# Five gathered columns of each run pass are fetched row by row from SyncE's queue

## The reference, cut to what matters

```python
pooled = jax.ops.segment_max(h[edge_src], edge_dst, num_segments=N)   # three times, first network
agg = jax.ops.segment_sum(msgs, dst, num_segments=n_nodes)            # two types of edge, third network
m = jax.ops.segment_sum(hW[edge_type, src], dst, num_segments=num_nodes)  # eight types, fourth network
```

## Time and profile before

| | |
|---|---|
| time, median of 3 runs | 4963.57 us (4955.61 to 4965.45) |
| the profiled execution's own time | 4973.72 us |
| its span | 4972.0 us |
| GpSimd busy | 3199.0 us (64% of the span) |
| VectorE busy | 2845.9 us (57%) |
| TensorE matmuls busy | 3481.2 us (70%) |

### The profile page before, as it was taken

The page is one execution under the profiler, slowest core; times in us unless marked ns, Lnnn a source line. Parts: engine busy times, 40 slices in busy tenths (PEclk is TensorE's granted clock), DMA queues, the critical chain, the costliest instruction groups (busy, mean ns, idle before and its releaser), DMA issues.

```text
span 4972.0 us, 70678 instructions
## 1 busy us (share of the span) xinstructions
PE 3481.2 (70%) x18022; PEld 2634.2 (53%) x18022; DVE 2845.9 (57%) x8726; ACT 2119.5 (43%) x4948; POOL 3199.0 (64%) x3257
## 2 busy tenths in 40 slices
PE   3122189979999688788888888887889987962100
PEld 2011178867788565556655565555778873431000
DVE  6754334436444688787888878787544442124433
ACT  1000068955788343335333353333479974420000
POOL 4777677766767377774777747776057772027776
PEclk7555599989999899999999999999999998985555
DMA  5556566665656433333333333333166662246665
GB/s 181 192 171 215 193 201 221 222 206 186 203 197 228 147 104 104 104 105 97 103 105 105 104 92 104 104 105 106 64 205 214 213 213 75 102 150 207 206 204 190
DMA packets 275492, 776.56 MB, mean 156 GB/s; under 512 B 63777, under 2 KB 99874, under 8 KB 270882
## 3 DMA queue, kind: packets, MB, share of 16 engines
q0 software_dynamic: 155568, 425.01, 29.9%
q1 hardware_dynamic: 119538, 347.03, 18.2%
HBM read 454.85 MB, written 316.93 MB: 155 GB/s over the span
## 4 chain that ended last, share of the span: by engine, by line
PE 34%; DMA 9%; POOL 9%; issue 6%; DVE 5%; ACT 2%; DVEq 1%; SPq 0%; POOLq 0%; ACTq 0%
PE PS L1157 9%; PE PS L1363 8%; POOL HC L539 5%; PE PS L1355 5%; PE PS L1289 3%; DMA X<-table,idx_src 3%; PE PS L1050 3%; DMA HC<-table_typ,run_typ 3%; DMA HC<-table,idx_src 2%; POOL HC L515 2%; POOL X L515 1%; DVE work L1985 1%; PE PS L1344 1%; PE PS L1452 1%; PE PS L1044 1%
## 5 line engine op out<-in xcount | busy, mean ns | idle before, releaser
L1798 DVE SCALAR_TENSOR_TENSOR HC<-HC,run_rst 128x256 f32<-128x256 f32 x1858 | 901.9, 485 | 930.3 <-DMA HC<-table,run_max 288.3
L539 POOL DMA_INDIRECT HC<-table,run_max x1101 | 1088.7, 989 | 462.2 <-issue 288.1
L515 POOL DMA_INDIRECT HC<-table,idx_src x648 | 639.1, 986 | 352.6 <-DMA table<-B 156.0
L1157 PE MATMUL PS<-AM,ring 128*128 128x256 f32 x3600 | 794.9, 384 | 26.7 <-ACT ring L738 21.9
L1157 PEld LDWEIGHTS PS<-AM,ring 128*128 128x128 f32 x3600 | 692.8, 193 | 129.0 <-DVE HC L1798 23.3
L515 POOL DMA_INDIRECT X<-table,idx_src x600 | 602.9, 1005 | 182.9 <-issue 128.0
L1355 PE MATMUL PS<-AM,work 128*128 x3744 | 648.8, 285 | 20.5 <-DVE score L1985 19.1
L2041 DVE SCALAR_TENSOR_TENSOR HC<-HC,fcol,PS 128x257 f32 x1248 | 586.0, 470 | 102.6 <-PE PS L1363 91.2
L539 POOL DMA_INDIRECT HC<-table_typ,run_typ x391 | 379.0, 969 | 396.2 <-DMA table_typ<-HC 277.3
L539 POOL DMA_INDIRECT HC<-table_rel,run_rel x371 | 360.6, 972 | 283.0 <-DMA table_rel<-B 170.2
L1355 PEld LDWEIGHTS PS<-AM,work 128*128 128x128 bf16 x3744 | 373.9, 101 | 224.2 <-issue 72.6
(11 more groups left out here) (270 smaller groups left out, 5640.2 us busy)
## 6 DMA issues: line engine op xcount, KB each, us to landing
prefix<-HC SPq DMA_DIRECT2D x485, 512.0 KB, 3.4
table_typ<-HC SPq DMA_DIRECT2D x18, 1024.0 KB, 3.8
HC<-table,run_max POOLq DMA_INDIRECT x1101, 3.3
HC<-table,idx_src POOLq DMA_INDIRECT x648, 2.8
X<-table,idx_src POOLq DMA_INDIRECT x600, 2.8
HC<-table_typ,run_typ POOLq DMA_INDIRECT x391, 2.9
table_typ<-AM SPq DMA_DIRECT2D x6, 1024.0 KB, 3.8
HC<-table_rel,run_rel POOLq DMA_INDIRECT x371, 3.3
```

Source lines behind the costliest of these rows:

```text
L515: pool.indirect_dma_start(held(t)[:, 0:D], None, table, bass.IndirectOffsetOnAxis(ap=idx_src[:, t:t + 1], axis=0)).then_inc(landed[t % AHE ...
L539: pool.indirect_dma_start(run_slot(k), None, src, bass.IndirectOffsetOnAxis(ap=run_idx[s[1]][:, j:j + 1], axis=0)).then_inc(landed[k], 16)
L1157: last = nc.tensor.matmul(PS[:, (2, 5)[c % 2], h * D:(h + 1) * D], duos(s)[:, x % 4, b % 2, h * P:(h + 1) * P], rows, start=(b + h == 0), ...
L1798: V.scalar_tensor_tensor(run_slot(k), run_slot((j - 1) % SLOTS), run_rst[:, j:j + 1], fresh, fade, join).then_inc(pooled, 1)
```

## The change

In every run stage, five columns (89, 162, 235, 308, 381) are no longer gathered by GpSimd. SP fetches each of them with 128 DMAs of one row, 1 KB, whose address in the table comes from a register. The registers are loaded 32 at a time from a list of row numbers that is kept on one partition. Seven such rows are issued ahead of each write of running rows, from turn 1 on, so a stage's 640 rows are out after 92 turns. A fetched column goes to one of three homes outside the 24 slots, and VectorE waits for its 128 landings, 16 counts each, before it combines it. For "rel" and "typ" SP loads two lists at the stage's start and VectorE computes the row numbers out of them with two small instructions before its first column.

```diff
+BY_SP = [89 + 73 * i for i in range(5)]
+BITE = 32
+A_TURN = 7
...
+def fetched_in(s):
+    return [] if s[0] != "runs" else BY_SP
...
+        def fetch(eng, n, rows, js, free):
+            s = PLAN[n]
+            for i, j in enumerate(js):
+                if i >= free:
+                    eng.wait_ge(pooled, before(n, ("runs",)) * TILES + js[i - free] + 1)
+                for p in range(0, P, BITE):
+                    regs = nc.values_load_multi_w_load_instructions(
+                        single_src[s[1]][0:1, bass.ds(fetched_in(s).index(j) * P + p, BITE)], engines=(eng.engine,), min_val=0,
+                        max_val=rows.shape[0] - 1, skip_runtime_bounds_check_because="the indices are the graph's own")[1]
+                    for k in range(BITE):
+                        eng.dma_start(single_home(s, j)[p + k:p + k + 1, :], rows[bass.ds(regs[k], 1), :]).then_inc(x_in[single_sem(j)], 16)
+                        yield
...
-                        if j in picked_in(s):
+                        if j in picked_in(s) + fetched_in(s):
                             continue
                         pool.indirect_dma_start(
...
+                    if s[1] == "rel":
+                        sp.wait_ge(rel_tabled[0], 16 * REL2 * 4)
+                        sp.wait_ge(rel_tabled[1], 16 * REL2 * 2)
+                    elif s[1] == "typ":
+                        for k in range(WIDES):
+                            sp.wait_ge(wided[k], ...)
+                    if s[1] != "max":
+                        kind = 1 if s[1] == "rel" else 2
+                        sp.dma_start(single_src[s[1]], singles[0:1, :]).then_inc(loaded, 16)
+                        sp.dma_start(single_type.bitcast(I32), singles[kind:kind + 1, :]).then_inc(loaded, 16)
+                    one_by_one = fetch(sp, n, {"max": table, "rel": table_rel, "typ": table_typ}[s[1]], BY_SP, 3)
                     for g in range(TURNS):
+                        if g == 1 and s[1] == "max":
+                            sp.wait_ge(loaded, 16 * 7)
+                            sp.wait_ge(tabled, 16 * PARTS * tables(n))
+                        elif g == 1:
+                            sp.wait_ge(keys_made, 2 if s[1] == "rel" else 3)
+                        if g >= 1:
+                            for _ in range(A_TURN):
+                                next(one_by_one, None)
                         while s[1] == "max" and far < len(pairs_in(s)) and pairs_in(s)[far][0] // 4 - 9 <= g:
...
+                        elif j in fetched_in(s):
+                            g = j // 4
+                            dve.wait_ge(written[g % TEAMS], 16 * (drained(n, g % TEAMS) + g // TEAMS))
+                            dve.wait_ge(x_in[single_sem(j)], x_count(n, single_sem(j), j))
+                            fresh = single_home(s, j)
```

More of the change, by code:

```diff
@@ L118, in duos_in, with gnn_kernel @@
     return -(-tabled_in(s) // 2)
-def gnn_kernel(nc, edges, runs, picks, rel_picks, xN, weights, biases, bias_rows, out, table, table_rel, table_typ, stash, step_rows, prefix):
+def fetched_in(s):
+    return [] if s[0] != "runs" else BY_SP
+def gnn_kernel(nc, edges, runs, picks, singles, rel_picks, xN, weights, biases, bias_rows, out, table, table_rel, table_typ, stash, step_rows, prefix):
     PLAN = plan()
@@ L252, in run_slot, with single_home, single_sem @@
             return flatC[:, k * D:(k + 1) * D]
+        single_src = {"max": Wfold[:].rearrange("p f c d -> p (f c d)")[0:1, 0:len(BY_SP) * P].bitcast(I32),
+                      "rel": AM[0:1, 35 * D:35 * D + len(BY_SP) * P].bitcast(I32)}
+        single_src["typ"] = single_src["rel"]
+        single_type = AM[0:1, 8 * D:8 * D + len(BY_SP) * P]
+        def single_home(s, j):
+            k = BY_SP.index(j) % 3
+            at = 32 * D if s[1] != "max" else 25 * D
+            return work[:, 1024 + k * D:1024 + (k + 1) * D] if s[:3] == ("runs", "max", 1) else AM[:, at + k * D:at + (k + 1) * D]
+        def single_sem(j):
+            return BY_SP.index(j) % 3
         def halves(v):
@@ L413, in columns, with x_count @@
         def columns(s, k, upto=TILES):
-            return sum(1 for j in range(k, upto, SLOTS) if j not in picked_in(s)) if k < SLOTS else 0
+            return sum(1 for j in range(k, upto, SLOTS) if j not in picked_in(s) + fetched_in(s)) if k < SLOTS else 0
+        def x_count(n, k, j=-1):
+            return 16 * sum({"start": 1, "attention": s[-1] == LAYERS - 1, "runs": P * sum(1 for f in fetched_in(s) if single_sem(f) == k)}.get(s[0], 0)
+                            for s in PLAN[:n]) + 16 * P * sum(1 for f in fetched_in(PLAN[n]) if single_sem(f) == k and f <= j)
         def own_bank(s, b):
@@ L522, in _ @@
                         pool.wait_ge(tabled, 16 * PARTS * tables(n))
-                        pool.wait_ge(loaded, 16 * 6)
+                        pool.wait_ge(loaded, 16 * 7)
                     elif s[1] == "rel":
@@ L586, in _ @@
                         sp.dma_start(part_in, runs[a]).then_inc(loaded, 16)
+                    sp.dma_start(single_src["max"], singles[0:1, 0:len(BY_SP) * P]).then_inc(loaded, 16)
                     sp.dma_start(bias[:], biases).then_inc(loaded, 16)
@@ L615, in _ @@
                     far = 0
-                    for g in range(TURNS):
+                    if s[1] == "rel":
[3 more added lines that the diff above has]
+                        for k in range(WIDES):
+                            sp.wait_ge(wided[k], 16 * (len(range(k, BLOCKS, WIDES)) + (3 if k == (BLOCKS - 1) % WIDES else 0)))
+                    if s[1] != "max":
[3 more added lines that the diff above has]
+                    one_by_one = fetch(sp, n, {"max": table, "rel": table_rel, "typ": table_typ}[s[1]], BY_SP, 3)
+                    for g in range(TURNS):
+                        if g == 1 and s[1] == "max":
[6 more added lines that the diff above has]
+                                next(one_by_one, None)
                         while s[1] == "max" and far < len(pairs_in(s)) and pairs_in(s)[far][0] // 4 - 9 <= g:
@@ L1720, in _ @@
                             centre(n, b, X[:, b, :], stage_in[:, b % TRS, :], t0 + b - TRS + 1 if b >= TRS else 0)
-                    dve.wait_ge(loaded, 16 * 6)
+                    dve.wait_ge(loaded, 16 * 7)
                     bi, hi = BIASES.index("bi"), BIASES.index("hi")
@@ L1779, in _ @@
                     if s[1] == "rel":
-                        dve.wait_ge(loaded, 16 * 8)
+                        dve.wait_ge(loaded, 16 * 9)
                         V.scalar_tensor_tensor(key_type, key_type.bitcast(I32), float(NODES), key_src, ALU.mult, ALU.add).then_inc(keys_made, 1)
+                    if not most:
+                        dve.wait_ge(loaded, 16 * (11 if s[1] == "rel" else 13))
+                        if s[1] == "rel":
+                            link(V.scalar_tensor_tensor(single_type, single_type.bitcast(I32), float(NODES), single_src["rel"], ALU.mult, ALU.add))
+                        else:
+                            link(V.scalar_tensor_tensor(single_type, single_src["typ"], float(REL8), single_type.bitcast(I32), ALU.mult, ALU.add))
+                        V.tensor_copy(single_src["rel"], single_type).then_inc(keys_made, 1)
                     work_inside = inside()
@@ L2098, in _ @@
                             if b % TRS == 0:
-                                dve.wait_ge(x_in[b // TRS], 32)
+                                dve.wait_ge(x_in[b // TRS], x_count(n, b // TRS))
                             ready[b] = mark(V.tensor_tensor(X[:, b, :], X[:, b, :], B[:, b, :], ALU.add))
@@ L2129, in picked_rows, with single_rows @@
             for a, pairs in ((2, PAIRS), (2, REL_PAIRS), (3, REL_PAIRS))]
+def single_rows(rows):
+    import numpy as np
+    return np.ascontiguousarray(rows[2:5, :, BY_SP].transpose(0, 2, 1).reshape(3, -1))
 def kernel(**inputs):
@@ L2181 @@
     picks, rel_picks = put("picks", picks[0]), put("rel_picks", np.stack([v.reshape(-1) for v in picks[1:]]))
-    args = [e, runs, picks, rel_picks, put("xN", xN), [put(f"w{i}", v) for i, v in enumerate(w)], put("bias_in", bias), put("bias_rows", rows)]
+    singles = put("singles", single_rows(by_run))
+    args = [e, runs, picks, singles, rel_picks, put("xN", xN), [put(f"w{i}", v) for i, v in enumerate(w)], put("bias_in", bias), put("bias_rows", rows)]
     args.append(nc.dram_tensor("outN", (P, BLOCKS, D), F32, kind="ExternalOutput").ap())
```

## The result

The changed kernel took 4938.95 us (median of 6 runs, 4933.94 to 4949.09), the kernel before 4960.35. The ratio is 0.9956, 95% interval 0.9946 to 0.9967. The two medians are 21.4 us apart, where 22.4 were forecast; the interval says 16 to 27. One of the six runs of the kernel before took 5224.10 us and is left out of the ratio; without it that median is 4957.14 and the difference 18.2 us. The profiled execution took 4938.62 us, its span 4936.9.

What follows compares the result with a forecast made beforehand. GpSimd's issue of gathers, 1.27 us a column, was taken as the bound, with TensorE's picks as slow in "max" 2 and 3. 28.4 - 1 - 5 = 22.4 us off 4963.6 gave 4941, range 4928 to 5110.

Steps and rivals of the forecast that it cites:

- What is removed: GpSimd, five gathers fewer per stage: 6.7, 5.1, 3.8, 6.4 and 6.4 us saved, 28.4 us in all.
- the rule that what is removed behind the last stall counts: "max" 2 and 3: only gathers removed after the last long stall for TensorE shorten the stage, 5.1 and 3.8 us.
- Gathers lengthened by the issues: -5: GpSimd's gathers beside SP's row issues: 0.0016 us a row, 1 us a stage, with 0 and 51 as bounds.
- the small DMA: A 32 KB DMA beside a gather, thought to leave it at 0.95 us; taken as nearer to a row than a write.
- Rival 3: GpSimd: the rows lengthen the gathers, +51 us a stage at 0.08 an issue, 5190 us in all; 15%.
- The price of a row: SP's time per one-row DMA, called c: 0.54 us taken, bounds 0.40 and 1.16, a turn of 4.25 to 4.34 us.
- rival 1: SP becomes the bound: beginning at c = 0.57 in "max" 2 and 3, deciding at about 0.62; slower; 20%.
- SP's lag: -1 in "max" 1: SP's writes, late after bursts: a lag of 5 to 8 us costs nothing; 1 us allowed behind "max" 1's stall.
- Rows in time: VectorE at fetched columns: last row issued about 12 columns, 15 us, ahead of use, so no waits.
- The starts of "rel" and "typ": Small loads and two VectorE operations delay VectorE's first column by 1 to 2 us, made good within three columns.
- Sum: Whole kernel: 28.4 - 1 - 5 = 22.4 us gained, forecast median 4941 us.
- The rules weighed: Two skill rules against the change: issuing from several engines saves next to nothing, and transfers under 64 KB are mostly overhead.

Runs made afterwards that it cites:

- the last set: Two kernels run against the kernel before at 4964.81 us: fixed-place rows added to all gathers (1.0006), and five columns neither gathered nor fetched (0.9939).
- the kernel with fixed rows and all gathers: Kernel before, all columns gathered, plus SP's 640 one-row transfers a stage from places fixed in the program, unused: 4967.91 us against 4964.81, ratio 1.0006.
- The kernel without rows: Kernel before with the five columns a stage neither gathered nor fetched, their rows missing from the result: 4936.95 us against 4964.81, ratio 0.9939.
- the slow sets: Three sets of ten experiments in which the kernel before took 6364 to 6460 us; the changed kernel, run in one, had ratio 0.9675.

## Why the prediction was right

**What is removed.** Forecast 28.4 us; 27.9 between the medians (0.9939, interval 0.9926 to 0.9953, so 23 to 37). This is the step that carries the forecast, and the two kernels of the last set show it: the removal gives the gain, rows of fixed places give none. By stage the split was less good. Against the kernel with fixed rows and all gathers, whose profiled execution was near its median, the changed kernel's stages ("max" 1, 2, 3, "rel", "typ") are shorter by 12.5, 2.0, -1.4, 7.8 and 7.1 us, 28.0 in all, where 6.7, 5.1, 3.8, 6.4 and 6.4 were forecast. The kernel without rows gives the same picture: 10.9, 4.3, -0.7, 6.6 and 5.5. "max" 1 gave nearly twice its term: 390.15 against 401.29 us of gathers, 11.1 for five of them, so the remaining 386 were shorter too (1.011 against 1.026 us each). Why isn't known; since the kernel without rows has it as well, it isn't the rows. "max" 3, with its stalls for TensorE, gave nothing by these comparisons and 4.7 by that with the kernel before; a single execution of each doesn't settle a term of 4 us there. So the rule that what is removed behind the last stall counts is not shown. The errors of size cancelled, and that the sum came out so close is in part luck.

**Gathers lengthened by the issues: -5.** The step chose the small DMA over the write as the nearest row to a one-row transfer, and it misread that row. The gather of the earlier trace rows ends at 3191.30 + 0.95 = 3192.25, and the issue begins at 3192.39: it lies in the gap between two gathers, not inside one. The trace of the kernel before has better ones. Of the 78 issues of line 677, 75 begin inside a gather, as here, and for 69 of them that gather lasted 0.95 us:

```profile
3254.31 0.95 POOL L515 DMA_INDIRECT HC<-table,idx_src  x1 [0.30 <-issue]
3255.57 1.07 POOL L515 DMA_INDIRECT HC<-table,idx_src  x1 [0.30 <-PE PS L1363]
...
3254.54 0.30 SPq L677 DMA_DIRECT2D work<-step_rows  x1
```

The gather that follows is the longer one, 1.16 us in the mean of the 75, and the trace doesn't tell why. So the choice was not secured by the rows, and that it held is luck as far as the evidence goes. The experiment is what secures it: fixed rows beside all gathers cost 3.1 us (interval -1.5 to 7.4, which takes in the 5), and no lengthening of gathers can be seen. Rival 3 asked for a mean of 0.985 in "typ" and got 0.962.

**The price of a row.** c = 0.50 in quiet groups and 0.53 by the means, against 0.54 taken, bounds 0.40 and 1.16. From row to row it was 0.41 to 0.45, a little under a burst's 0.47 with the register operation in it; the index load's median of 2.2 us is the 2 x 1.10 of the forecast, its mean of 2.45 a little more. Rows of fixed places went out 0.30 us apart in the median, the 302 ns of the earlier trace rows, so an address in a register costs 0.11. At 4960 us rival 1 (c over 0.57) did not come true, though in the slow sets, at a mean of 0.82 from row to row, its mechanism is plain.

**SP's lag: -1 in "max" 1.** GpSimd's waits for writes grew by 10.8 us, and "max" 3 alone has 11.5 us in 8 waits, next to its stalls for picks. They were placed wrongly. What they cost there is within the uncertainty of that stage; the kernel without rows, without such waits in "max" 3, has that stage at 469.40 against 470.10.

**Rows in time.** No wait of VectorE for a row. The starts of "rel" and "typ" were mis-sized: 11.3 and 3.8 us against 1 to 2. VectorE made it good, as argued: "rel" is 8.7 us shorter than in the kernel before.

**Sum.** 27.9 for the removal, less 3.1 for the rows' issue, is 24.8; measured 18 to 21, interval 16 to 27. The difference may be the index loads and the addresses in registers, or nothing: the kernel before had medians of 4960.35 and 4964.81 in the two sets.

**The rules weighed.** The Trainium skill's section "Issuing engines are not separate DMA queues" on the page "DMA: Bandwidth & Descriptors" calls the issuing sequencer's time usually small beside the transfer. Here it was the bound, and moving it to another engine was worth 0.44%: the measurement decides against it for a stage that GpSimd's issue limits. The rule against transfers under 64 KB in the Trainium skill's section "Rules for kernel authors" on the same page agrees as to who pays: 128 transfers of 1 KB cost SP 64 to 68 us for a column that one gather brings at 1.27. It only pays since SP had 2237.1 us to wait.

## What to carry to other kernels

An engine that issues indirect transfers one after the other is relieved by as much as each issue costs it, if another engine's queue stands still anyway. Price that other queue by its full turn, with the index loads in it, against the shortest turn of the stage. Where stalls for a second engine come in the stage, take the term for what is removed as good to some microseconds at most. Run the extra work and the removal each alone: here 1.0006 and 0.9939 say more than any stage of one trace, in which 0.5% more or less in the mean gather of a stage went with no change in the time. And look into the trace of an experiment for what it is said to contain: here the index loads that one of them was named for were not in it.

## What the runs showed of the hardware

A one-row transfer is issued by SP every 0.30 us if its address is fixed in the program and every 0.41 us if it is in a register (medians; means 0.37 and 0.45). An index load of 32 values holds SP 2.0 to 3.3 us, 2.2 in the median. In the changed kernel GpSimd's mean gather in "typ" was 0.962 us with all of this beside it, against 0.969 without.

The same kernel can take 6364 to 6460 us in place of 4961 to 4965, with waits of up to 17.8 us on TensorE that the profile puts down to nothing of the program. A gather costs there what it costs elsewhere; the mean distance of row issues doubles. There a change of 0.44% measured as 3.25%, and rows that add work and take none away as 2.8% in its favour. Whoever measures a change should look at the absolute time of the kernel before, too, before believing a ratio.
